# Eight places of a four-layer transformer on one core: more products of the identity on TensorE, and layer 3's output pieces half a step sooner

## What is computed

```python
x = x + jnp.tanh(g_xattn[0]) * _L0_xattn_ref(ctx_2048, ctx_2048, _layernorm(x, axis=-1), L0_xattn_ssm_kernel, L0_xattn_D, 8)
x = x + jnp.tanh(g_ffn[0]) * _L0_ffn_ref(_layernorm(x, axis=-1), ...)
...
x = x + jnp.tanh(g_xattn[3]) * _L3_xattn_ref(_layernorm(x, axis=-1), ctx_2048, ctx_2048, L3_xattn_gamma)
x = x + jnp.tanh(g_ffn[3]) * _L3_ffn_ref(_layernorm(x, axis=-1), L3_ffn_factors, L3_ffn_bias)
```

```python
qk = jnp.einsum('bhdq,bhdl->bhql', qh, kh) * scale
sm = jax.nn.softmax(qk, axis=-1)
ret = jnp.einsum('bhql,bhdl->bhdq', sm, vh)
```

## Time and profile before

| | |
|---|---|
| median of 3 runs | 2333.96 us (2329.02 to 2335.72) |
| the profiled execution | 2334.76 us; its span from first to last instruction 2332.9 us |
| PE busy | 2137.0 us (92%) |
| DVE busy | 1876.3 us (80%) |
| ACT busy | 1351.3 us (58%) |
| POOL busy | 1303.1 us (56%) |
| mean granted TensorE clock | 0.974 |

### The profile page before, as it was taken

The page is one execution under the profiler, slowest core; times in us unless marked ns, Lnnn a source line. Parts: engine busy times, 40 slices in busy tenths (PEclk is TensorE's granted clock), DMA queues, the critical chain, the costliest instruction groups (busy, mean ns, idle before and its releaser), DMA issues. The chain is left out here.

```text
span 2332.9 us, 43643 instructions
## 1 busy us (share of the span) xinstructions
PE 2137.0 (92%) x14464; PEld 1780.4 (76%) x14464; DVE 1876.3 (80%) x3850; ACT 1351.3 (58%) x3408; POOL 1303.1 (56%) x1970
## 2 busy tenths in 40 slices
PE   5989999899999988999998899999899999569997
PEld 2368888789888877888887788887788888346665
DVE  5865687699999988999998677777587887788887
ACT  2213454688888877887885433333344545677765
POOL 4913344288999978999997211110344544654443
PEclk9999999999999999999999999999799999898999
DMA  4211021310000020000000400001000000001100
GB/s 135 84 39 72 38 86 55 127 35 18 12 17 15 24 82 14 20 17 17 19 6 1 132 22 21 28 21 44 23 8 8 8 6 2 1 27 46 35 29 19
DMA packets 39933, 82.39 MB, mean 35 GB/s; under 512 B 6048, under 2 KB 25824, under 8 KB 35776
## 3 DMA queue, kind: packets, MB, share of 16 engines
q1 hardware_dynamic: 39712, 79.60, 10.2%
HBM read 67.00 MB, written 12.58 MB: 34 GB/s over the span
## 5 line engine op out<-in xcount | busy, mean ns | idle before, releaser
L1535 PE MATMUL bank<-l_wr,l_xq 128*128 128x256 f32 (+1 forms) x1024 | 214.1, 352 | 6.9 <-ACT l_raw L1641 5.7
L910 PE MATMUL bank<-m_xr,m_wgr 128*128 128x512 f32 x864 | 211.3, 394 | 2.1 <-DVE m_xr L1031 2.1
L910 PEld LDWEIGHTS bank<-m_xr,m_wgr 128*128 128x128 f32 x864 | 158.6, 190 | 32.6 <-issue 2.6
L1852 POOL TENSOR_TENSOR l_tiny<-l_tiny,l_minus_half 128x6 f32<-128x6 f32 x128 | 175.9, 1375 | 10.7
L1535 PEld LDWEIGHTS bank<-l_wr,l_xq 128*128 128x128 f32 x1024 | 158.9, 192 | 24.9 <-issue 8.0
L1655 ACT ACTIVATE xn_T<-bank,l_head_b,l_head_w 128x512 f32<-128x512 f32 x128 | 99.6, 778 | 128.5 <-PE bank L1583 128.5
L828 POOL TENSOR_TENSOR m_wgr<-m_wg,m_wgr 128x512 fp32r<-128x512 f32 x18 | 23.3, 1294 | 261.7 <-ACT m_wgr L817 261.7
L1572 PE MATMUL bank<-l_wpr,l_cat 128*128 128x256 f32 x1024 | 167.6, 306 | 0.8 <-POOL l_cat L1901 0.8
L1238 POOL TENSOR_SCALAR l_stage<-l_stage,l_means,l_full_scale 128x128 f32<-128x128 f32 x80 | 71.4, 903 | 159.4 <-DVE l_means L1225 159.4
L1550 PE MATMUL bank<-xn_T 128*128 128x128 f32 x1024 | 141.8, 282 | 18.8 <-ACT xn_T L1627 17.3
L2736 ACT ACTIVATE l_pr<-bank,l_negmax 128x256 f32<-128x256 f32 x256 | 117.8, 473 | 65.5 <-DVE l_negmax L2768 65.5
(11 more groups left out here) (377 smaller groups left out, 6396.0 us busy)
## 6 DMA issues: line engine op xcount, KB each, us to landing
l_stage<-in_l_w SPq DMA_DIRECT2D x8, 1024.0 KB, 4.8
l_xs<-l_saved SPq DMA_DIRECT2D x25, 256.0 KB, 2.6
l_centred<-l_stage SPq DMA_DIRECT2D x6, 1024.0 KB, 3.9
l_stage<-l_centred SPq DMA_DIRECT2D x6, 1024.0 KB, 4.8
m_unsplit<-in_m_w SPq DMA_DIRECT2D x14, 384.0 KB, 3.3
m_wg<-in_m_gu SPq DMA_DIRECT2D x18, 256.0 KB, 2.6
x_norm<-in_ctxT_b SPq DMA_DIRECT2D x32, 128.0 KB, 2.0
l_stage<-in_l_wp SPq DMA_DIRECT2D x4, 1024.0 KB, 4.7
```

What stands on the lines that cost most here:

```text
L910: r = e.matmul(banks[2 * (n % 2) + half][:, :], WGR[:, u % 2, a, k, half, :], XR[:, b, k, cols], start=k == 0 and m == 0, stop=k == KT - 1 ...
L1535: r = e.matmul(to, XQ[:, q % 2, v, k, :], WR[:, j, part, k, h0 * P:h1 * P], start=k == 0 and part == 0, stop=k == KT - 1 and part == 1)
L1852: pool_own.did(e.tensor_tensor(r0, var, minus_half[:, :], ALU.pow))
```

## The change

Products of the identity are added in seven places: one after each batch's transposes in two layernorms (L0 from batch 4 on, L2 from batch 2 on), 5 more at the end of L0's attention, 6 and 8 at the fronts of the MoEs, 12 and 7 in L1's steps 13 and 15, and 14 and 16 in L3's first step and near its end. In L3, SyncE issues the first context ahead of the three small loads. In L3's loop TensorE's `turn_x` goes from the odd steps to the end of the even step before, and `project` from the end of the odd step to behind `values`; VectorE's `norm_out` goes ahead of the two copies of its even step, `keep_x` to the front of the odd step, and `add_out` from the next even step to the end of the odd one.

```diff
-        def layernorm(ends, kind="once", transposed=True, counted=True, beside=None, load_root=True, between=None, ring=4):
+        def layernorm(ends, kind="once", transposed=True, counted=True, beside=None, load_root=True, between=None, ring=4, warm_from=None):
...
                     r.then_inc(turned.sem, 1)
+                    if warm_from is not None and b >= warm_from:
+                        warm(e, banks[7], 1)
...
-            ends = layernorm(ends, load_root=False) + [loaded(2)]
+            ends = layernorm(ends, load_root=False, warm_from=4) + [loaded(2)]
...
-                warm(e, banks[7], 30)
+                warm(e, banks[7], 35)
...
                     turn(e, b, 0)
+                warm(e, banks[7], 6)
                 route_matmul(e, 0, 0)
...
                 turn(e, 1)
+                warm(e, banks[2], 8)
                 up_project(e, 0)
...
                         project(e, s - 13)
+                    if s in (13, 15):
+                        warm(e, pscore, 12 if s == 13 else 7)
...
-            ends = layernorm(ends, ring=2, between=keep_values) + [loaded(n_loaded), put(4), put_q(1), segf(1)]
+            ends = layernorm(ends, ring=2, between=keep_values, warm_from=2) + [loaded(n_loaded), put(4), put_q(1), segf(1)]
...
                 begin(e, load_ends)
+                e.dma_start(CK[:, 0, :], A["ctx"][0]).then_inc(s_ck.of(0), 16)
                 e.dma_start(even[:, :], A["l3_even"]).then_inc(loaded.sem, 16)
...
                         score(e, s, 1)
+                    if s == 0:
+                        warm(e, pacc[0], 14)
                     if 1 <= s <= N:
                         turn(e, s - 1, 0)
-                    if s >= 5 and s % 2 == 1:
-                        turn_x(e, (s - 5) // 2)
                     if 1 <= s <= N:
                         turn(e, s - 1, 1)
                     if 2 <= s < N + 2:
                         values(e, s - 2)
+                    if s >= 5 and s % 2 == 1:
+                        project(e, (s - 5) // 2)
...
-                    if s >= 5 and s % 2 == 1:
-                        project(e, (s - 5) // 2)
+                    if s == N + 2:
+                        warm(e, scores[0], 16)
+                    if s >= 4 and s % 2 == 0:
+                        turn_x(e, (s - 4) // 2)
...
-                for s in range(N + 5):
+                for s in range(N + 4):
...
-                    if s >= 6 and s % 2 == 0:
-                        add_out(e, (s - 6) // 2)
+                    if s >= 5 and s % 2 == 1:
+                        keep_x(e, (s - 5) // 2)
...
-                    if s >= 5 and s % 2 == 1:
-                        keep_x(e, (s - 5) // 2)
...
+                    if s >= 4 and s % 2 == 0:
+                        norm_out(e, (s - 4) // 2)
                     if 1 <= s <= N:
                         keep_turned(e, s - 1, 2)
                     if 1 <= s <= N:
                         keep_turned(e, s - 1, 3)
-                    if s >= 4 and s % 2 == 0 and s < N + 4:
-                        norm_out(e, (s - 4) // 2)
+                    if s >= 5 and s % 2 == 1:
+                        add_out(e, (s - 5) // 2)
```

More of the change, by code:

```diff
@@ L2583, in l3_attention @@
             load_ends = ends
+            s_ck = Slots(signals, "ctx_loaded", B, 16, 2)
+            s_ct = Slots(signals, "l3_ct_loaded", B, 16, 2)
             def load(e):
                 begin(e, load_ends)
+                e.dma_start(CK[:, 0, :], A["ctx"][0]).then_inc(s_ck.of(0), 16)
                 e.dma_start(even[:, :], A["l3_even"]).then_inc(loaded.sem, 16)
@@ L2597, in l3_attention @@
             gamma = signals("l3_gamma_ready", 1)
-            s_ck = Slots(signals, "ctx_loaded", B, 16, 2)
-            s_ct = Slots(signals, "l3_ct_loaded", B, 16, 2)
             s_xn = signals("l3_xn", B)
@@ L2630, in sync @@
                         e.wait_ge(*s_score(4 * (b - 1)))
-                    e.dma_start(CK[:, b % 2, :], A["ctx"][b]).then_inc(s_ck.of(b), 16)
+                    if b >= 1:
+                        e.dma_start(CK[:, b % 2, :], A["ctx"][b]).then_inc(s_ck.of(b), 16)
                     if b >= 2:
```

## The result

The changed kernel took 2316.97 us (2313.76 to 2319.96, 6 executions) beside 2334.39 us (2328.81 to 2341.18, 6) of the kernel before: ratio 0.9927, interval 0.9909 to 0.9946, so it is faster by 0.7%, beyond its interval. The medians over all executions of the changed kernel (both occasions) and of the kernel before (all occasions) are 2319.4 us (16) and 2332.2 us (68): 12.8 us. I take the gain to be 12 to 17 us; 19.7 was forecast, for a time of 2315.

What follows compares the result with a forecast made beforehand. The prediction took TensorE, 92% busy and at half clock behind pauses, as the bound, with L3's loop held by TensorE and VectorE waiting for each other. Eight terms summed to -19.7 us, from 2334.8 to 2315 us, range 2304 to 2327.

Steps and rivals of the forecast that it cites:

- L1's front: L1's steps 13 and 15: 7 products delay turn_heads, partly showing; +0.6 us, bounds 0 and +1.8.
- L3's front: L3's first steps: 14 products in the 3.46 us wait bring the first values sooner; -2.8 us, bounds 0 and -3.3.
- L3's end: Last half batch and projection: no turn_x ahead of values, -0.7, and 16 products in a wait, -1.2; -1.9 us.
- L0's layernorm: L0's transposes: a product per batch from batch 4 delays the first convolution; +2.1 us, bounds +1.0 to +2.7.
- First MoE: Around the first router: products in waits hold the clock through 149.9 to 156.7; -2.5 us, bounds 0 and -3.4.
- Second MoE: First projection: eight products fit the 2.15 us wait and the clock holds; -1.4 us.
- L2's front: L2's layernorm up to the second query: products hold the clock; -6.0 us, bounds +2.8 and -10.
- L3's loop: L3's loop: the new order makes a period 13.05 us instead of 13.65, 13 times; -7.8 us, bounds 0 and -13.7.
- (2): Fronts of L2 and first MoE: clock doesn't hold where transposes are half the records; -8.4, 2326 us; chance 0.15.
- (3): L3's loop gains nothing, the turn_x wait being as long as the two it replaces; -11.9, 2323 us; chance 0.12.
- (6): L3's loop: slower if GpSimd's root for norm_out comes late, 1.5 us per period beyond the walk; chance 0.04.
- the rule on transposes: Fronts made of transposes: the skill says transposes don't count as busy for the clock; the forecast followed the trace instead.

Runs made afterwards that it cites:

- e1: The kernel before with only the new order of L3's loop, no added products; ratio to before 0.9959.
- e9: The kernel before with only turn_x, norm_out and keep_x moved in L3's loop, project and add_out left in place; ratio to before 1.0021.
- e7: The changed kernel with L2's remaining waits filled: 4 products behind the layernorm, 2 before the first keys, 7 before the second query; ratio to before 0.9945.
- e4: The changed kernel without the products in L2's layernorm; ratio to before 0.9944.
- e12: e8 without the products in L2's layernorm, the 4 behind it kept; 2307.00 us, ratio to before 0.9909.
- e8: The changed kernel with the additions of e6, e7 and e10 together and L1's 7 products of step 15 removed; 2305.55 us, ratio to before 0.9889.
- e5: The changed kernel run again, unchanged; ratio to before 0.9955.
- e6: The changed kernel with 22 products behind L0's layernorm instead of one after each batch in it; ratio to before 0.9944.
- e10: The changed kernel with 3, 2 and 5 more products in three waits of L3's first two steps; 2316.96 us, ratio to before 0.9947.
- e11: The changed kernel without the 14 products of L3's first step; 2319.62 us, ratio to before 0.9960.
- e2: The changed kernel with L3's loop in the old order, all added products kept; ratio to before 0.9991.
- e3: The changed kernel without the products in L0's layernorm; ratio to before 0.9932.

## Why the prediction was right, and where it was not

The time (2317 against 2315) and the sign came out. Five of the eight terms have about the right size; L1's front, L3's front and L3's end are off by a factor of about two. By its own steps, with the lengths of the table (mean over the traces that have the code in question, less the mean of before, e1 and e9 where those have the old code):

- **L0's layernorm, +2.1**: +2.4 (34.1 against 31.7). It was a pure cost, and the low clock behind the pause stayed, as said.
- **First MoE, -2.5**: 8.9 against 11.0, -2.1. In ten of eleven traces it is 9.0 or 9.1, since the clock still fell, but later (153.8 instead of 149.9), as said; in e7's it didn't fall there, 7.5.
- **Second MoE, -1.4**: 6.5 against 8.3, -1.8; the 12 records took 3.00 us.
- **L1's front, +0.6**: 19.9 against 18.6, +1.3. `turn_heads` came 2.2 us later, as said; more of it showed than the 0.6 taken near the lower end, within the bounds 0 and +1.8.
- **L2's front, -6.0**: 312.5 to 317.6, mean 314.1, against 320.0 is -5.9. That this met the forecast is luck: single traces of this code give -2.4 to -7.5, and the reason was not shown. The step was that the products hold the clock through the layernorm since they more than double the records there; e4, e1 and e12 show transposes holding it alone. The low stretch of the earlier trace rows didn't begin behind a pause either, as the prediction had read it: at 1631.3 us TensorE was among the layernorm's transposes, with gaps of 0.28 us. What the length of L2 does follow is how long the clock is low in it: 311.9 to 312.2 us with no low clock (e7, e8, e12), 312.5 to 312.7 with 3.4 us of it (e5, e6, e10, e11), 315.2 to 315.5 with 10.2 (changed, e2, e4), 317.6 with 17 (e3), and 318.9, 320.4 and 320.8 with 20, 27 and 31 (e1, before, e9). So the gain is a shorter low clock. What makes it shorter in the traces with other products than in the three without any stays open; it comes and goes between executions of one code, and three traces are few.
- **L3's front, -2.8**: 22.5 against 23.9, -1.4, the term that was too large. I went through the first three steps as if they ran at full clock throughout; the pauses between them (0.69, 0.59 and 1.07 us) were left empty, and the clock fell behind the last. Where it stayed full (e6, e10) the front is 20.5, 3.4 shorter, which is the 3.3 of that walk. The first context, said to bring nothing, cost a little: VectorE's first work waits 1.00 us for `l_gam` instead of 0.49, and starts 4.0 us after the last statistics in all eleven traces with the context first, 3.5 in the three without; the first scores start 5.8 instead of 5.6 us after them.
- **L3's loop, -7.8**: 199.1 against 206.3, -7.2 (without e3, whose low clock reaches into it). The period was to be 13.05 and is 13.08, from the walk. Where the new wait stands was wrong: not 0.7 at `turn_x` but 0.42 one `turn` earlier, for ScalarE. When that wait ends, `norm_out` (done at 2150.63) is there too, and `turn_x` starts at 2150.69.
- **L3's end, -1.9**: 8.0 against 8.8, -0.8, too large. e1 with the order alone still needs 8.8 us, so the 0.7 for `values` no longer behind a `turn_x` brought nothing. The 16 products brought the rest, but end before the last wait (1.18 us at `turn_x`, 0.52 behind it), and the last projection took 1.69 us, not 1.03.

Their sum is -15.5 us, inside the 12 to 17 that the runs give. Of the rivals, (2) is excluded by the changed kernel's own fronts: its clock is full until 1638.6 us in L2 and until 153.8 us in the first MoE. (3) is excluded by the period and by e1. (6), the late root, did not happen, but e9 shows its place: with the wait at `turn_x` and the old one both in a period, the kernel is slower, 1.0021.

The argument against the rule on transposes rested on the earlier trace rows, the durations of weight loads. The granted clock doesn't show that rise: the profile prints 1.00 for 20.0 to 23.6 us of that trace as well. That transposes hold a full clock is shown by e4's window; that they raise it rests on those durations alone.

## What to carry to other kernels

Where two engines hand work to one another in a loop, walk one period through both in the new order and add up: it gave 13.05 us for 13.08, while moving only half of the pieces made the loop slower. Fill pauses of TensorE up to the moment when the next operand comes, not the stretches in which it already works: in L0 the products inside the layernorm cost some 2.5 us and kept no clock behind it, and to have 22 behind it in their place brought the next stage 4.5 us sooner. In L2 it isn't settled whether those inside do anything. And judge a filling by several executions, since one trace may show a fall of the clock that the next one doesn't have.

## What the runs showed that I had not expected

The place and length of the low clock differ between executions of identical code at identical waits: 10.2 us or nothing in L2's front (the changed kernel and e5), and 6.8 or 30.7 us in L3's (the changed kernel and e3, whose code there is the same). In the 30.7 us TensorE was busy without a break. Transposes hold the full clock (1.00 over 7.45 us in e4) while TensorE is busy 5.50 of them. And the kernel before spread from 2323.5 to 2341.2 us over 68 executions. In the 62 beside the experiments the shortest had a mean granted clock of 0.981, the longest (2340.1 us) 0.970: 16.6 us go with a hundredth of the clock.
